# First loads on two queues, first unit's adapters inside the second unit, halves and last block reordered

## The chip, the cores and the metric

The kernel runs on one core of one Trainium2 chip. The metric is the device time of one execution in microseconds (us), from the first instruction to the last with what lies around them; lower is better. The engines are called here as in the profile: PE (TensorE, matmuls), DVE (VectorE), ACT (ScalarE), POOL (GpSimd) and SP (SyncE, which only begins transfers). ACT's queue can begin transfers too.

## The reference

```python
# x: (8, 256, 1024) float32; adapters chosen per sequence by itok_B_2_6 and itok_B_1_7
def lora_add(base, inp, A, B):                     # rank 16
    t = einsum('bri,bni->bnr', A[0][lora_indices], inp)
    return base + einsum('bor,bnr->bno', B[0][lora_indices], t) * 0.5
gate = lora_add(einsum('bnh,fh->bnf', x, W_gate), x, A_gate, B_gate)   # F = 2752
up   = lora_add(einsum('bnh,fh->bnf', x, W_up),   x, A_up,   B_up)
act  = silu(gate) * up
x = x + lora_add(einsum('bnf,hf->bnh', act, W_down), act, A_down, B_down)
x = x + einsum('bsi,oi->bso', x, weight) + bias + scale * lora(x)      # 1024 x 1024
```

## The kernel before

All products are float32 made of pairs: each operand is split into a high part (ACT writes it, rounded to the matmul's type) and a low part (DVE or POOL subtract the high part from the source), and PE multiplies high*high, high*low and low*high. So before a product can start, its weights (`W`) and its tokens (`X_B`, `X_T`) must have been loaded, turned by a DVE transpose, copied by ACT and subtracted by DVE or POOL.

The first phase makes `act`. The 2048 tokens go in two halves of 1024; each half runs over 22 units of 128 features (the last has 64). Twenty of the units of a half save products by sums and differences of quarter blocks (stages P1 to P7), for which DVE makes sums of tokens (`T1` to `T4`, `x_sum`) and of weights. The first two units of a half are multiplied plainly, since these sums aren't there yet: `first_unit` (banks a, b, c, d for gate and up, and both chunks of 512 tokens, with the tokens in two parts kq = 0 and 1 as they arrive) and `second_unit`. The first unit also multiplies the adapters' A matrices (`AG`) with the tokens. From that come the small matrices `Tm_g` and `Tm_u`: ACT copies one part (`t_copy`), DVE adds the other and masks (`t_sum`), ACT makes high parts (`t_high`), DVE low parts (`t_low`). The adapter stages E11, E21, E12 and E22 multiply them with `Bf` and close the banks. In the first unit these four stages come right behind its last product.

The tiles are loaded by SP into three rotating buffers `raw` in one written order (`raw_order`). A load waits until the item three places earlier has been turned, and takes 4 to 16 transfers: 4 for an x tile (`("x", half, n)`) or a gate or up tile (`("G", U)`, `("U", U)`), 16 for one pair of adapters A (`("Ag", half, p)`), 8 for B (`("b", half, n)`). SP also reads the adapters' indices from memory one by one (`batch_indices`); the eight indices and eight scale factors of the last layer are read behind `("b", 0, 0)`.

The second phase multiplies `act` with `W_down` in 11 blocks; in each block every pair of banks is added by DVE to `acc` (`add_down`). Before a pair can be multiplied again, its add must be done: (k, pr) is feature tile k for half pr, `t` the down adapters' A product. In the last block the adapters B (`Bd`, four of them; the last two serve the second half) and `Td` close each pair. The third phase multiplies with `weight` and stores; the last result's second chunk is stored by SP in 4 transfers.

PE, DVE, ACT and POOL each run their own instructions in the order in which the functions below issue them, and wait for each other by semaphores; nothing is reordered by a scheduler. In the rows L1843 is the matmul helper, L475 turns a weight tile, L536 an x tile, L581 a pair of A adapters, L592 a B tile, L567 is `x_sum`, L571 and L1729 are the low parts of tokens, L1725 the low part of weights, L613 and L616 `t_sum`, L1403 `t_high`, L622 `t_low`, L604 `b_low`, L821 and L832 turn and split `Bd`, L886 is the add of a bank pair, L904 `td_low`.

## Time and profile before

| | |
|---|---|
| median of 3 runs | 1707.95 us (1706.78 to 1709.65) |
| the profiled execution's own time | 1708.54 us |
| its span, first to last instruction | 1706.7 us |
| PE busy | 1631.3 us, 96% of the span |
| DVE busy | 1126.1 us, 66% |
| POOL busy | 668.2 us, 39% |
| ACT busy | 501.5 us, 29% |
| mean granted clock of PE | 0.985 of full speed |

The span is that of the profiled execution; 1.8 us of its time lie around it. Busy shares are means over the whole span. The page also cuts the span into 40 slices: PE is 90% busy or more in 35 of them, and below that in the first two, at the change of halves, near the last block and in the last one.

### The profile page before, as it was taken

The page shows a single profiled execution, that of the slowest core. Times are in us where ns is not written, and L with a number is a line of the kernel's source. Part 1 is how long each engine was busy: PE and PEld are TensorE (multiplying, and loading weights), DVE is VectorE, ACT ScalarE, POOL GpSimd, SP SyncE. Part 2 cuts the span into 40 slices and gives each one's busy share as a digit, 9 for nine tenths or more (in the row PEclk, how much of TensorE's full clock was granted, in tenths as well). Part 3 has the DMA queues.
Part 4 walks back from the last instruction along what each step waited for, and adds up shares of the span by engine and source line. Part 5 has one row for each costly group of instructions (what it writes and reads, how often), then busy time and mean ns, then how long its engine had stood idle before and what let it go on. Part 6 is the DMA issues. An engine that isn't in the chain of part 4 may idle for free.

```text
span 1706.7 us, 20952 instructions
## 1 busy us (share of the span) xinstructions
PE 1631.3 (96%) x7060; PEld 1320.1 (77%) x7060; DVE 1126.1 (66%) x1294; ACT 501.5 (29%) x833; POOL 668.2 (39%) x449
## 2 busy tenths in 40 slices
PE   4499999999997999999999999999999999899998
PEld 3378788888876788888888788888888887678886
DVE  3767777777768677777777565665555577765343
ACT  2343333333334433333433311111111122331100
POOL 3254444444444544444444533333233331541110
PEclk9799999999998999999999999999999999999999
DMA  6224344533442234335332662222222130103322
GB/s 132 60 78 102 103 126 113 149 88 92 113 111 67 77 103 125 116 102 163 91 90 89 177 221 78 77 78 60 68 76 78 58 69 25 25 21 78 74 46 59
DMA packets 218318, 156.13 MB, mean 91 GB/s; under 512 B 110884, under 2 KB 200356, under 8 KB 215460
## 3 DMA queue, kind: packets, MB, share of 16 engines
q1 hardware_dynamic: 171872, 115.97, 26.7%
q10 hardware_dynamic: 46212, 38.81, 7.1%
q8 instruction: 58, 0.95, 0.2%
q14 instruction: 48, 0.39, 0.1%
q0 software_dynamic: 128, 0.00, 0.0%
HBM read 115.38 MB, written 39.32 MB: 91 GB/s over the span
## 4 chain that ended last, share of the span: by engine, by line
PE 61%; DVE 2%; issue 1%; POOL 1%; ACT 0%; DMA 0%; SPq 0%; ACTq 0%; DVEq 0%
PE ps L1843 61%; POOL act L1768 0%; DVE acc L886 0%; POOL Wd L1776 0%; DMA raw<-in_x_dram 0%; POOL W L1725 0%; DVE tw_down L860 0%; DVE turned L821 0%; DVE tw_down L869 0%; DVE act_last L892 0%; DVE tw_down L899 0%; ACT W L1300 0%; DVE s L508 0%; DVE tw_down L866 0%; DVE tw_down L863 0%
## 5 line engine op out<-in xcount | busy, mean ns | idle before, releaser
L1843 PE MATMUL ps<-act,Wd 128*128 128x512 f32 x2016 | 463.3, 390 | 2.3 <-DVE acc L886 1.2
L1843 PE MATMUL ps<-X_T,W 128*128 128x512 f32 x1944 | 460.1, 392 | 5.6 <-DVE X_T L571 3.8
L1843 PE MATMUL ps<-X_B,W 128*128 128x512 f32 x1728 | 424.8, 395 | 22.2 <-POOL W L1725 15.3
L1843 PEld LDWEIGHTS ps<-act,Wd 128*128 128x128 f32 x2016 | 379.1, 188 | 83.0 <-DVE acc L886 1.6
L1843 PEld LDWEIGHTS ps<-X_T,W 128*128 128x128 f32 x1944 | 364.2, 188 | 89.1 <-DVE vbuf L636 8.2
L1843 PEld LDWEIGHTS ps<-X_B,W 128*128 128x128 f32 x1728 | 329.5, 191 | 96.2 <-POOL W L1725 14.2
L886 DVE TENSOR_TENSOR acc<-acc,ps 128x1024 f32<-128x1024 f32 x176 | 214.3, 1220 | 186.8 <-PE ps L1843 186.3
L1725 POOL TENSOR_TENSOR W<-s,W 128x512 fp32r<-128x512 f32 x156 | 208.8, 1339 | 237.9 <-ACT W L1300 237.9
L1725 POOL TENSOR_TENSOR W<-TG,W 128x512 fp32r<-128x512 f32 x88 | 131.8, 1499 | 205.8 <-ACT W L1300 205.8
L1300 ACT ACTIVATE W<-s 128x512 fp32r<-128x512 f32 x156 | 98.7, 632 | 281.0 <-PE ps L1843 275.3
L1768 POOL TENSOR_TENSOR act<-stage,act 128x1024 fp32r<-128x1024 f32 x42 | 100.6, 2415 | 175.2 <-ACT act L1518 175.2
L1843 PE MATMUL ps<-X1hi,Wo 128*128 128x512 f32 x512 | 141.4, 390 | 0.0
L1843 PEld LDWEIGHTS ps<-X1hi,Wo 128*128 128x128 f32 x512 | 96.1, 188 | 20.6
L1518 ACT ACTIVATE act<-stage 128x1024 fp32r<-128x1024 f32 x42 | 42.4, 1049 | 186.1 <-PE ps L1843 165.3
L630 DVE TENSOR_TENSOR qbuf<-p1buf,ps 128x512 f32<-128x512 f32 x38 | 26.1, 688 | 106.1 <-PE ps L1843 105.9
L1776 POOL TENSOR_TENSOR Wd<-turned,Wd 128x512 fp32r<-128x512 f32 x44 | 55.8, 1292 | 73.9 <-ACT Wd L1552 73.9
L1300 ACT ACTIVATE W<-TG 128x512 fp32r<-128x512 f32 x88 | 55.0, 628 | 88.1 <-PE ps L1843 78.4
L1843 PE MATMUL ps<-X1lo,Wo 128*128 128x512 f32 x256 | 80.3, 390 | 0.0
L604 DVE TENSOR_TENSOR Bf<-ts,Bf 32x256 fp32r<-32x256 f32 (+1 forms) x88 | 62.4, 709 | 26.3 <-ACT Bf L1384 24.4
L1725 POOL TENSOR_TENSOR W<-TU,W 128x512 fp32r<-128x512 f32 x46 | 60.5, 1318 | 38.6 <-ACT W L1300 38.6
L1384 ACT ACTIVATE Bf<-ts 32x256 fp32r<-32x256 f32 (+1 forms) x176 | 71.8, 408 | 1.5
L1776 POOL TENSOR_TENSOR Wo<-turned,Wo 128x512 fp32r<-128x512 f32 x16 | 21.8, 1380 | 120.8 <-ACT Wo L1552 120.8
(131 smaller groups left out, 1541.7 us busy)
## 6 DMA issues: line engine op xcount, KB each, us to landing
raw<-in_L_cond_W_gate_dram SPq DMA_DIRECT2D x168, 128.0 KB, 3.2
raw<-in_L_cond_W_up_dram SPq DMA_DIRECT2D x168, 128.0 KB, 3.2
stage<-act_scratch SPq DMA_DIRECT2D x21, 1024.0 KB, 5.1
raw<-in_x_dram SPq DMA_DIRECT2D x128, 128.0 KB, 3.2
raw<-in_L_cond_W_down_dram SPq DMA_DIRECT2D x88, 128.0 KB, 3.3
act_scratch<-c21buf ACTq DMA_DIRECT2D x42, 256.0 KB, 2.4
act_scratch<-vbuf ACTq DMA_DIRECT2D x42, 256.0 KB, 2.8
xt_scratch<-xt ACTq DMA_DIRECT2D x4, 2048.0 KB, 7.1
```

What stands on the lines that cost most here:

```text
L604: last = V.tensor_tensor(dst, src, hi.bitcast(F32), ALU.subtract)
L630: V.tensor_tensor(qbuf[:, :], p1buf[:, :], bank(U % 2, "b"), ALU.add).then_inc(q_done, 1)
L886: V.tensor_tensor(acc[pr][:, k, :], acc[pr][:, k, :], src[:, :], ALU.add).then_inc(b_added.up(s), 1)
L1300: A.activation(hi, src, ACT.Copy).then_inc(w_hi, 1)
L1384: last = A.activation(home, src, ACT.Copy)
L1518: A.activation(acts[t % 3][:, 0, cols], stage[t % 2][:, cols], ACT.Copy).then_inc(act_hi.up((t, pr)), 1)
L1725: G.tensor_tensor(low, src, hi.bitcast(F32), ALU.subtract).then_inc(w_lo, 1)
L1768: G.tensor_tensor(acts[t % 3][:, 1, cols], stage[t % 2][:, cols], acts[t % 3][:, 0, cols].bitcast(F32), ALU.subtract).then_inc(act_lo.up(( ...
L1776: last = G.tensor_tensor(low, src, hi.bitcast(F32), ALU.subtract)
L1843: return nc.tensor.matmul(dst, stationary, moving, start=start, stop=stop, skip_group_check=True)
```

## The change

The diff does the following.

- First loads: tiles G and U of unit 0 get buffers of their own (`raw_first`, where `Tm` lies later) and are begun by ACT's queue, while SP begins x tiles 0 to 3; the pair `("Ag", 0, 0)` comes behind them. For half 0 an A pair is loaded by 4 transfers of whole rows (4 KB a row) in place of 16 (1 KB a row), and DVE turns it by 8 transposes of 32 partitions in place of one of 128. SP reads only the two indices that it needs next, and the reads and loads for the last layer's factors move from behind `("b", 0, 0)` to behind `("b", 0, 3)`.
- First unit: its stages E11, E21, E12 and E22 are issued within the second unit, behind that unit's stage I11. `tw` holds both chunks, so that ACT copies both at once. DVE does all `t_sum` and then all `t_low`, and the first unit's silu and product with up (`plain_acts`) come in the second unit, on ACT behind the T4 tokens.
- Change of halves: x tiles 6 and 7 of half 1 are loaded and turned behind the half tile, in the first unit; x tiles 4 and 5 are turned behind `add_c12`; ACT does `copy_p1` ahead of `silu_second`.
- Last block: `Bd` 2 and 3 are turned and split within the last block rather than in and behind the block before it; `last_low(1)`, `td_first` and the turning of `Wo` and `Al` move as well.
- Last store: SP and ACT begin two of its four transfers each.

```diff
+        raw_first = {"G": at("raw_gate", 190464, [P, 1024]), "U": at("raw_up", 194560, [P, 1024])}
-        tw = at("tw", 180224, [Q, 2, TT])
+        tw = at("tw", 180224, [Q, 2, 2, TT])
...
-            order = [("x", 0, 0), ("x", 0, 1), ("G", 0), ("U", 0), ("Ag", 0, 0), ("x", 0, 2), ("x", 0, 3)]
+            order = [("x", 0, 0), ("x", 0, 1), ("x", 0, 2), ("x", 0, 3), ("Ag", 0, 0)]
...
+                    if h == 1:
+                        order += [("x", 1, 6), ("x", 1, 7)]
+                    order += [("Ag", h, 1)]
...
+                for w in range(2):
+                    for q in range(NQ):
+                        last = V.transpose(
+                            ts[q * Q:(q + 1) * Q, :].rearrange("p (k w i) -> p k w i", k=KT, w=2)[:, :, w, :],
+                            src[w * Q:(w + 1) * Q, q * HQ:(q + 1) * HQ].rearrange("p (k i) -> p k i", k=KT))
...
             def first_unit(U):
...
                 turn_tile(("U", U + 1))
+                b_low(U)
                 x_low(h, "T1", 0)
                 x_sum(h, "T1", 1)
+                for p in range(2):
+                    for w in range(2):
+                        t_sum(h, p, w)
+                for p in range(2):
+                    for w in range(2):
+                        t_low(h, p, w)
...
                 b_low(U + 1)
-                plain_acts(U)

             def second_unit(U):
                 h = U // UNITS
+                plain_acts(U - 1)
...
             def down_block(bb):
...
-                    elif bb == BLOCKS - 2 and n == 12:
+                    elif bb == BLOCKS - 2 and n == 11:
                         last_low(0)
-                        turn_item(("Bd", 2))
-                        bd_low(2)
-                    elif bb == BLOCKS - 2 and n == 14:
-                        turn_item(("Bd", 3))
-                    elif bb == BLOCKS - 2 and n in (15, 16):
-                        td_first(n - 15)
+                    elif bb == BLOCKS - 2 and n in (14, 15):
+                        td_first(n - 14)
 
             def last_block():
-                last_low(1)
-                bd_low(3)
                 for s in B_CLOSE[-18:]:
                     _, k, pr = s
                     add_down(s)
                     if (k, pr) == ("t", 0):
                         td_low(0, 0)
                         td_low(0, 1)
+                    elif (k, pr) == (0, 0):
+                        last_low(1)
+                    elif (k, pr) in ((1, 0), (3, 0)):
+                        turn_item(("Bd", 2 + k // 2))
+                    elif (k, pr) in ((2, 0), (4, 0)):
+                        bd_low(1 + k // 2)
...
         @block.scalar
         def _(eng):
             A = nc.scalar
...
+            for kind, w in (("G", w_gate), ("U", w_up)):
+                rows = w.rearrange("(g i) m -> i g m", i=Q)
+                for c in range(NQ):
+                    eng.dma_start(raw_first[kind][c * Q:(c + 1) * Q, :].rearrange("i (q m) -> i q m", q=NQ),
+                                  rows[:, 0:2 * NQ:2, c * HQ:(c + 1) * HQ]).then_inc(first_full[kind], 16)
...
                 x_high(h, "T2", 0)
+                b_high(U)
                 x_high(h, "T1", 1)
                 t_copy(h, 0)
-                b_high(U)
+                t_copy(h, 1)
                 t_high(h, 0)
-                x_high(h, "T2", 1)
-                t_copy(h, 1)
-                t_high(h, 1)
                 w_high(U + 1, "A11")
                 w_high(U + 1, "A12")
+                t_high(h, 1)
+                w_high(U + 1, "A21")
+                w_high(U + 1, "A22")
+                b_high(U + 1)
+                x_high(h, "T2", 1)
...
         @block.tensor
...
+            def first_adapters(U):
+                a, b, c, d = (bank(U % 2, n) for n in "abcd")
                 up(U, "E11", adapter(U, 0, 0, a))
                 up(U, "E21", adapter(U, 1, 0, b))
                 up(U, "E12", adapter(U, 0, 1, c))
...
                 both_chunks(U, 1, 1, (a, c))
+                first_adapters(U - 1)
                 both_chunks(U, 1, 2, (a, c))
```

How the order of instructions moves is seen on PE at the end of the first unit. `X_B` and `X_T` are tokens, `W_58` to `W_61` the four weight buffers, `Bf_82`/`Bf_84` and `Bf_83`/`Bf_85` the B adapters of the even and the odd units (numbered 82, 83 before and 84, 85 now). Before:

```order
L1843 MATMUL ps<-X_T_54,W_60 128x512 x6
L1843 MATMUL ps<-X_B_52,W_61 128x512 x6
L1843 MATMUL ps<-Tm_g,Bf_82 128x512
L1843 MATMUL ps<-Tm_u,Bf_82 128x512
L1843 MATMUL ps<-Tm_g,Bf_82 128x512
L1843 MATMUL ps<-Tm_u,Bf_82 128x512
L1843 MATMUL ps<-X_B_49,W_58 128x512 x12
L1843 MATMUL ps<-X_T_54,W_58 128x512 x12
L1843 MATMUL ps<-X_B_50,W_59 128x512 x12
L1843 MATMUL ps<-X_B_52,W_59 128x512 x12
```

And now:

```order
L1884 MATMUL ps<-X_T_54,W_60 128x512 x6
L1884 MATMUL ps<-X_B_52,W_61 128x512 x6
L1884 MATMUL ps<-X_B_49,W_58 128x512 x12
L1884 MATMUL ps<-X_T_54,W_58 128x512 x12
L1884 MATMUL ps<-Tm_g,Bf_84 128x512
L1884 MATMUL ps<-Tm_u,Bf_84 128x512
L1884 MATMUL ps<-Tm_g,Bf_84 128x512
L1884 MATMUL ps<-Tm_u,Bf_84 128x512
L1884 MATMUL ps<-X_B_50,W_59 128x512 x12
L1884 MATMUL ps<-X_B_52,W_59 128x512 x12
```

The four adapter products with `Tm` stood between the first unit's last product and the second unit's first; now 24 matmuls of the second unit's first weight tile (`W_58`) stand ahead of them.

On DVE the work around the start of the last block, before (`tw_down` with `ps` is the add of the first half's adapter product, `acc_87` is written by the last adds of the block ahead of it):

```order
L821 STREAM_TRANSPOSE turned_97<-raw_67 32x32x32
L886 TENSOR_TENSOR acc_87<-acc_87,ps 128x1024
L899 TENSOR_TENSOR tw_down<-tw_down,tacc 32x1024
L886 TENSOR_TENSOR acc_87<-acc_87,ps 128x1024
L899 TENSOR_TENSOR tw_down<-tw_down,tacc 32x1024
L886 TENSOR_TENSOR acc_87<-acc_87,ps 128x1024
L892 TENSOR_TENSOR act_last<-stage_89,act_last 64x1024
L832 TENSOR_TENSOR Bd_108<-turned_97,Bd_108 32x4x8x32
L860 TENSOR_TENSOR tw_down<-tw_down,ps 32x512
L863 TENSOR_TENSOR tw_down<-tw_down,ps 32x512
L869 TENSOR_TENSOR tw_down<-tw_down,pick_half 32x512
L860 TENSOR_TENSOR tw_down<-tw_down,ps 32x512
```

And now, from the add of (0, 0) to the second half's adapter product (`acc_88` is written by the first half's adds):

```order
L909 TENSOR_TENSOR acc_88<-acc_88,ps 128x1024
L915 TENSOR_TENSOR act_last<-stage_91,act_last 64x1024
L909 TENSOR_TENSOR acc_88<-acc_88,ps 128x1024
L844 STREAM_TRANSPOSE turned_98<-raw_67 32x32x32
L909 TENSOR_TENSOR acc_88<-acc_88,ps 128x1024
L855 TENSOR_TENSOR Bd_109<-turned_98,Bd_109 32x4x8x32
L909 TENSOR_TENSOR acc_88<-acc_88,ps 128x1024
L844 STREAM_TRANSPOSE turned_99<-raw_68 32x32x32
L909 TENSOR_TENSOR acc_88<-acc_88,ps 128x1024
L855 TENSOR_TENSOR Bd_110<-turned_99,Bd_110 32x4x8x32
L883 TENSOR_TENSOR tw_down<-tw_down,ps 32x512
L886 TENSOR_TENSOR tw_down<-tw_down,ps 32x512
```

The second low part of `act_last` and the transposes and low parts of the last two `Bd` stood ahead of the first half's adapter product; now they stand between the adds of the last block, ahead of the second half's adapter product.

## Rows read from the trace of the kernel before

**Rows 1.** Waits of the matmul engine over the span: us in total, times, longest:

```profile
PE ps L1843 <- DVE Tm_g L622: 26.2, 3, 11.9
PE ps L1843 <- POOL W L1725: 15.3, 3, 14.2
```

**Rows 2.** Timeline of PE, 0 to 125: start us, us busy, instructions, [idle before <-releaser]:

```profile
14.23 7.98 PE L1843 MATMUL ps<-X_B,W 128*128 128x512 f32 x24 [14.23 <-POOL W L1725]
...
58.88 1.52 PE L1843 MATMUL ps<-X_B,W 128*128 128x512 f32 x6
...
83.76 4.61 PE L1843 MATMUL ps<-X_B,W 128*128 128x512 f32 x12 [0.52 <-POOL W L1725]
...
98.36 0.73 PE L1843 MATMUL ps<-Tm_g,Bf 96*128 96x512 f32 x2 [1.83 <-DVE Bf L604]
...
110.33 2.93 PE L1843 MATMUL ps<-X_B,W 128*128 128x512 f32 x12
```

**Rows 3.** Timeline of the SP queue, 0 to 60:

```profile
13.45 3.85 SPq L1140 DMA_DIRECT2D raw<-in_L_cond_A_gate_dram  x8
...
53.02 5.13 SPq L1241 DMA_DIRECT2D scale_row<-ond_scaling_factors_dram  x8
```

**Rows 4.** Page, DMA issues: count, KB each, median us from issue to landing:

```profile
raw<-in_x_dram SPq DMA_DIRECT2D x128, 128.0 KB, 3.2
```

**Rows 5.** Busy time by window, DMA share in the last place but one:

```profile
4.00:12.00 8.00, 0.00 (x0) 0.00 (x0) 3.79 (x4) 2.02 (x3) 0.77 (x5) 1.00 1.11 212
```

**Rows 6.** Timeline of DVE, 0 to 70:

```profile
8.41 1.25 DVE L536 STREAM_TRANSPOSE xt<-raw 128x1024 f32<-128x1024 f32 x1 [1.56 <-DMA raw<-in_x_dram]
...
46.81 1.25 DVE L475 STREAM_TRANSPOSE TG<-raw 128x1024 f32<-128x1024 f32 x1 [0.99 <-DMA raw<-in_L_cond_W_gate_dram]
...
53.73 1.21 DVE L592 STREAM_TRANSPOSE ts<-raw 64x256 f32<-64x256 f32 x2
62.45 1.25 DVE L475 STREAM_TRANSPOSE TU<-raw 128x1024 f32<-128x1024 f32 x1 [7.51 <-DMA raw<-in_L_cond_W_up_dram]
...
67.71 0.68 DVE L613 TENSOR_TENSOR tw<-tw,ps 32x512 f32<-32x512 f32 x1 [0.47 <-ACT tw L1394]
```

**Rows 7.** Timeline of ACT, 50 to 75:

```profile
69.91 0.63 ACT L1403 ACTIVATE Tm_g<-tw 32x512 fp32r<-32x512 f32 x1
```

**Rows 8.** Timeline of POOL, 30 to 85:

```profile
32.30 2.46 POOL L1729 TENSOR_TENSOR X_B<-xt,X_B 128x1024 fp32r<-128x1024 f32 x1 [6.94 <-ACT X_B L1329]
...
82.35 3.49 POOL L1725 TENSOR_TENSOR W<-TG,W 128x512 fp32r<-128x512 f32 x2 [29.63 <-ACT W L1300]
```

**Rows 9.** Timeline of PE at the change of halves:

```profile
499.46 4.61 PE L1843 MATMUL ps<-X_B,W 128*128 128x512 f32 x12 [2.05 <-ACT p1buf L1337]
...
551.93 4.37 PE L1843 MATMUL ps<-X_B,W 128*128 128x512 f32 x12 [0.52 <-POOL W L1725]
...
577.42 2.93 PE L1843 MATMUL ps<-X_B,W 128*128 128x512 f32 x12
```

**Rows 10.** Timeline of DVE at the change of halves:

```profile
522.81 1.25 DVE L475 STREAM_TRANSPOSE TG<-raw 128x1024 f32<-128x1024 f32 x1 [0.16 <-DMA raw<-in_L_cond_W_gate_dram]
```

**Rows 11.** Timeline of PE in the last block:

```profile
1459.07 0.47 PE L1843 MATMUL ps<-Td,Bd 96*128 96x512 f32 x1 [3.70 <-DVE Td L904]
...
1460.87 2.76 PE L1843 MATMUL ps<-act,Wd 128*128 128x512 f32 x6
...
1480.42 1.64 PE L1843 MATMUL ps<-act,Wd 128*128 128x512 f32 x6 [1.21 <-DVE acc L886]
```

**Rows 12.** Timeline of DVE before and in the last block:

```profile
1420.18 3.98 DVE L845 STREAM_TRANSPOSE Ad_turned<-Ad_raw 32x64 f32<-32x64 f32 x16
...
1436.13 2.08 DVE L821 STREAM_TRANSPOSE turned<-raw 32x1024 f32<-32x1024 f32 x1
...
1461.11 1.22 DVE L886 TENSOR_TENSOR acc<-acc,ps 128x1024 f32<-128x1024 f32 x1 [0.89 <-PE ps L1843]
```

**Rows 13.** Timeline of the SP queue, last stores:

```profile
1702.32 1.99 SPq L439 DMA_DIRECT2D out_dram<-ct  x4
```

More of the change, by code:

```diff
@@ L210, in last_stage @@
         def last_stage(U):
-            return (U, stages_of(U % UNITS)[-1])
-        STAGES = [(U, s) for U in range(ALL) for s in stages_of(U % UNITS)]
+            return (U, "E22" if plain(U) else stages_of(U % UNITS)[-1])
+        STAGES = []
+        for U in range(ALL):
+            for s in stages_of(U % UNITS):
+                STAGES += [(U - 1, e) for e in ("E11", "E21", "E12", "E22")] if s == "first" else [(U, s)]
         pe_a = Order("pe_a", STAGES)
@@ L257, in raw_order @@
                 if h == 0 and u == FULL - 1:
-                    order += [("G", U + 2)] + [("x", 1, n) for n in range(4, 8)]
+                    order += [("G", U + 2), ("x", 1, 4), ("x", 1, 5)]
                 if h == 0 and u == FULL:
@@ L279, in dmas @@
                 return 8
-            if item[0] in ("Ag", "Al"):
-                return 16 if item[0] == "Ag" else 32
+            if item[0] == "Al":
+                return 32
+            if item[0] == "Ag" and item[1] == 1:
+                return 16
             return 8 if item[0] == "G" and half_tile(item[1]) else 4
@@ L430, in b_places, with store_out @@
             return src, homes[0], homes[1]
-        def store_out(eng, m, c):
+        def store_out(eng, m, c, qs=range(NQ)):
             k, pr = divmod(m, 2)
             eng.wait_ge(out_turned, (k // 2 * 2 + pr) * 2 + c + 1)
-            for q in range(NQ):
+            for q in qs:
                 col = q * HQ + (k - 1) * Q
@@ L460, in turn_tile @@
                 kind, U = item
-                src = take(item)
+                if U == 0:
+                    eng.wait_ge(first_full[kind], NQ * 16)
+                    src = raw_first[kind]
+                else:
+                    src = take(item)
                 if kind == "G":
@@ L1086, in _, with batch_indices @@
         def _(sp):
-            def batch_indices(table, rows):
-                return [sp.value_load(indices[:, table * NB + b:table * NB + b + 1], min_val=0, max_val=rows - 1)
-                        for b in range(NB)]
+            l0, l1 = {}, {}
+            def batch_indices(table, batches):
+                found, rows = ((l0, a_gate.shape[1]), (l1, a_out.shape[0]))[table]
+                for b in batches:
+                    found[b] = sp.value_load(indices[:, table * NB + b:table * NB + b + 1], min_val=0,
+                                             max_val=rows - 1)
             def slot(item):
@@ L1138, in load_ag @@
                         rows = a_all[bass.ds(l0[h * 4 + 2 * p + b], 1), :, :].rearrange("o r m -> (o r) m")
+                        if h == 0:
+                            first = w * Q + b * R
+                            sp.dma_start(buf[first:first + R, :], rows).then_inc(filled, 16)
+                            continue
                         for q in range(NQ):
@@ L1232, in _ @@
                         sp.wait_ge(indices_loaded, 2 * 16)
-                        l0 = batch_indices(0, a_gate.shape[1])
+                    first = 4 * item[1] + 2 * item[2]
+                    batch_indices(0, range(first, first + 2))
                     load_ag(item)
@@ L1268, in _ @@
                     load_bo(item)
-            store_out(sp, 2 * KT - 1, 1)
+            store_out(sp, 2 * KT - 1, 1, range(0, 2))
             for c in range(2):
@@ L1388, in t_copy @@
                 wait_stage(eng, h * UNITS, f"A{p}")
-                if p == 1:
-                    eng.wait_ge(t_lo, 4 * h + 2)
-                elif h == 1:
-                    eng.wait_ge(act2_done, UNITS)
+                if h == 1:
+                    for c in range(2):
+                        eng.wait_ge(act_stored[c], 16 * UNITS)
                 for w in range(2):
-                    A.activation(tw[:, w, :], bank(1, "dc"[p])[(2 * w + 1) * Q:(2 * w + 2) * Q, :], ACT.Copy
+                    A.activation(tw[:, p, w, :], bank(1, "dc"[p])[(2 * w + 1) * Q:(2 * w + 2) * Q, :], ACT.Copy
                                  ).then_inc(t_copied, 1)
@@ L1691, in _ @@
                         store_out(eng, m, 1)
+                    else:
+                        store_out(eng, m, 1, range(2, NQ))
                 if pr == 1 and k + 2 < KT:
```

94 lines of the change are left out of this document (45 added, 49 removed).

## The prediction

> **What bounds the kernel now.** I read the waits of PE first, then PE's timeline where they fall, then the queue and the engine that PE waited for there. The matmuls keep PE busy for nearly the whole span; what can still be won is idle time and half-clock time, and it lies in four places. The longest waits are for `Tm_g`, 26.2 us in three waits, and for weights, 15.3 us in three [rows 1]. On the timeline: PE starts at 14.23; the last product of the first unit ends at 60.4 (58.88 + 1.52); the second unit starts only at 83.76, and the third at 110.33 [rows 2]. A unit there is 100 matmuls, some 23 us at full clock, since 12 in the third unit take 2.93 and the last overlaps the next (about 0.23 each). In the same place of the second half the second unit starts at 551.93 and the third at 577.42 [rows 9]. In the last block PE waits 3.70 for `Td`, then runs slowly (6 matmuls in 2.76 rather than 1.4), and waits once more at 1480.42, 1.21 for an add of DVE [rows 11]. Last come four stores begun one behind the other in 1.99 [rows 13].
>
> **The first loads.** SP and ACT would begin loads at once. The window from 4 to 12 has a DMA share of 1.11 and 212 GB/s [rows 5]: the sixteen DMA engines are full already. x tiles 0 and 1 and tiles G and U are 2 MB, 9.9 us at that rate, whichever queue begins them. So x tile 1, turned at 8.41 before [rows 6], now shares the engines with G and U and lands somewhere between there and 12; I take 11, because two queues with equal shares leave it until nearly the end of the 2 MB. The Trainium skill says the same (DMA: Bandwidth & Descriptors, "Issuing engines are not separate DMA queues"): transfers begun by several engines interleave on the same sixteen, and only issue time is saved. By that rule alone this edit gives nothing; by the row it costs 2 to 3 us at PE's start (14.23, now about 16.5), and gives it back only if what comes behind is earlier.
>
> What comes behind hangs on DVE. From 11 it does seven operations of 1.2 (1.25 for a tile [rows 6]): x1, G, a low part, U, a low part, x2, x3: 19.5. Then the A pair in 8 pieces. Sixteen pieces of 64 columns take 3.98, 0.25 each [rows 12]; two of 256 columns take 1.21, 0.6 each [rows 6]; one instruction for all can't be under half a tile's 1.25. That bounds the eight by 0.6 and 4.8; I take 3.3, between the two piece rows: 22.8. ACT's three copies (0.63 for 512 columns [rows 7], so an estimated 1.1 for 1024) bring 25.6; POOL now does a token low part first, 2.46 [rows 8], then AG's 1.3: 29.3. The second pair waits for that, since both use `ts`: 32.6. Now SP loads x6, x7 and G of unit 1: 12 transfers at 0.48 (8 in 3.85 [rows 3]) and 3.2 to land [rows 4] make 41.5. Before, DVE turned that G at 46.81 [rows 6]. This step is 5.3 us earlier.
>
> **From G of unit 1 to its first product.** DVE turns G, makes two token sums and turns B: 46.81 to 54.94, 8.1 us [rows 6]. I keep that: 49.6. Before, DVE then sat 7.51 until U landed at 62.45, behind the eight scale factors, 5.13 of SP's queue [rows 3, 6], and their index reads. Those are now behind `b` 3, and U (begun by about 45) is there. From U to the first product was 21.3 us (62.45 to 83.76), because `tw` held one chunk: the second chunk's copy, sum, mask, high and low parts came behind the first's, and W's high part behind them all on ACT. Now: U 1.2, `b_low` with its wait 1.3, two token operations 2.4, ACT's high part and first copy 1.7, four small DVE operations at 0.7 [rows 6] 2.8, the last two high parts 1.3 and W's 0.6 [rows 7], W's low part 1.7 (3.49 for two [rows 8]): 13.0. The second unit starts at 62.6 rather than 83.76, 21.2 earlier. PE's first unit ends before that: x7 is turned at about 41, two low parts of POOL (2.5 or more each) last to 47, and 32 matmuls behind them, 7.4, end at about 55. So it still idles 7 us and starts at half clock, as the 4.61 for 12 matmuls shows for now too [rows 2].
>
> **The rest of the second unit.** Before, it took 26.6 (83.76 to 110.33). The four adapters lie in it now (0.9), and PE then waits for `b_low` of unit 1, as it did for 1.83 at 98.36 [rows 2]: DVE has the same sums and one or two low parts more ahead of it, so some 15 us from the unit's start where it was 14.6. From there to the third unit are 12.0 (98.36 to 110.33). That gives 26.9; the third unit starts at 89.5, 20.8 earlier. The silu and product of unit 0 have moved into this unit, ahead of the next unit's weight sums, and `b_high` now ends about 3 us later against the third unit. By my count the add that its stage P7 needs is 2.1 late. 18.7 are left.
>
> **The change of halves.** x tiles 6 and 7 no longer stand ahead of `second_act`, and `p1buf` is copied first: PE's 2.05 wait and the half clock behind it (4.61 for 12 rather than 2.93) go [rows 9]. But the path that decides is DVE's again: G of the second unit is turned at 522.81 [rows 10]; it can be perhaps 1 earlier, since SP's order of loads up to it is the same. From there 8.1 and 13.0, as above, give 542.9 rather than 551.93, then 26.9: 569.8 against 577.42 [rows 9], 7.6 earlier. P7 loses 0.7: 6.9.
>
> **The last block.** The 3.70, the half clock and some waits go, since DVE has only the adapter product's six operations ahead of `Td`. PE arrives at (0, 1) at about 1472.5. That product needs the add of (5, 0), and DVE now does in between, from 1455.9: six adds of 1.22, `last_low` 1.2, two `Bd` transposes of 2.08 [rows 12], their low parts 2.4, two waits of 1.1 for ACT's part, and six small operations 4.3: 21.6. So PE waits until 1477.5 where it went on at 1480.42 [rows 11], and after 5 us of idleness it again runs at half clock; the present stretch lost 1.4 on 6 matmuls [rows 11], so some 2.4 altogether. Gain 0.6. The stall moves.
>
> The Trainium skill's clock rule (TensorE: Matmul & The Clock Gate, "Part 1: The HAM clock gate") puts PE at 1.2 GHz after idling and back at 2.4 GHz when busy. It would leave this gain at 0.6; without it the gain would be 3.0.
>
> **The last store.** Two transfers on SP rather than four: 1.0 [rows 13].
>
> **The sum.** 18.7 + 6.9 + 0.6 + 1.0 = 27.2. The profiled execution took 1708.5, 0.6 over the median of the three runs, so 1681.3.
>
> **Rivals.**
> 1. More is won. For: x1 lands at 9, the A pair turns in 2 rather than 3.3 (twice), P7 doesn't wait (2.8) and the last block loses no clock (2.4). 2 + 2.6 + 2.8 + 2.4 = 9.8 gives 1671.5. Against: each is a wait that I could derive from rows. 0.2.
> 2. The Vector path is longer. x1 at 12, eight pieces at 0.6 (3 us for both pairs), token sums slowed by POOL's low parts by 2 at each half, and the waits at P7 longer than 2 so that they too end in half clock (1.7 each): 1 + 3 + 4 + 3.4 = 11.4 gives 1692.7. For it: from 46.81 to 54.94 lie three operations that elsewhere take 1.25 and the B pair's 1.21 [rows 6], 5.0 in all, and they took 8.1, so DVE is slowed beside others here. 0.2.
> 3. The loads give nothing and only the order does: the step of 5.3 is lost, 1686.6. This lies in the forecast's own range. The Trainium skill's sentence above points this way.
> 4. Slower than before: the 38 ordinary units get longer, because every later load lies in another of the three `raw` buffers and the factor loads (some 10 us of queue with their reads) now come in unit 5. It needs 0.7 us in each unit to eat 27; the factors alone could cost at most their own 10, once. Nothing in the rows sets one buffer apart, and the queue idles most of a unit. 0.03, and 0.02 for no change.
> The forecast, 1675 to 1689, has 0.55.
>
> **The range.** With rivals 1 and 2 to their middles, 1671 to 1694. Differences under 0.2% (3.4 us) of this kernel can't be told from none.
>
> **What the new profile would show.** PE's first matmul later than 14.23, by about 2; x1 turned at about 11; the second unit's first product at 60 to 66 and the third unit at 87 to 94; waits of PE for `Tm` near zero and a wait for W of some 7 in their place; a wait at the third unit's fourth stage; no wait for `Td`, but one of 4 to 6 for an add of DVE near 1450, and half clock behind it; the ordinary units as before. I am wrong if PE waits for A products beyond 30, if the second unit starts after 70, or if the last block's wait is gone.

## The result, and the profile after

The changed kernel took 1692.10 us (median of four runs, 1689.88 to 1692.88) against 1707.59 for the kernel before (four runs): ratio 0.9905, 95% interval 0.9888 to 0.9923. That is 15.5 us less where the sum gave 27.2. It is inside the range of 1671 to 1694, but 10.8 above the number and above the 1675 to 1689 to which the forecast had given 0.55. The profiled executions, on which the rest goes, stand at 1708.54 and 1689.88, their spans at 1706.7 and 1688.1: 18.6 less. The profiled one is the fastest of the four. In three of the runs below (`ag_four`, `one_queue`, `ends_back`), in which PE, DVE and ACT keep this stretch's order, PE waited 2.1 at P7 and went on at half clock, where this trace has 0.49 and full clock; whether the three slower executions of the changed kernel did the same is not shown, since they have no trace. "Half clock" is PE's granted clock of 1.2 GHz in place of 2.4: 12 matmuls take 2.9 us at full clock and up to 5.5 (at 529.81 below, granted clock 0.50) where the clock is half.

PE's waits in the changed kernel, by line and by what ended them (total, times, longest):

```profile
PE ps L1884 <- POOL W L1763: 30.0, 3, 16.7
PE ps L1884 <- POOL AG L1772: 7.1, 2, 5.9
PE ps L1884 <- DVE acc L909: 6.1, 2, 5.5
PE ps L1884 <- DVE Bf L627: 3.7, 2, 2.3
PE ps L1884 <- DVE X_B L585: 1.9, 1, 1.9
...
PE ps L1884 <- DVE qbuf L653: 1.4, 2, 0.9
PE ps L1884 <- DVE vbuf L659: 1.3, 2, 0.7
```

The 26.2 for `Tm` [rows 1] are gone and the waits for W are 30.0 rather than 15.3. There is a small wait for `qbuf`, the add that stage P7 needs, in each half; the forecast had charged it with 2.1 and 0.7. PE's timeline of the start:

```profile
64.20 4.58 PE L1884 MATMUL ps<-X_B,W 128*128 128x512 f32 x12 [8.23 <-POOL W L1763]
...
80.21 0.74 PE L1884 MATMUL ps<-Tm_g,Bf 96*128 96x512 f32 x2 [2.31 <-DVE Bf L627]
80.79 4.51 PE L1884 MATMUL ps<-X_B,W 128*128 128x512 f32 x12
...
93.78 2.93 PE L1884 MATMUL ps<-X_B,W 128*128 128x512 f32 x12
...
102.64 3.01 PE L1884 MATMUL ps<-X_T,W 128*128 128x512 f32 x12 [0.49 <-DVE qbuf L653]
...
109.49 3.06 PE L1884 MATMUL ps<-X_T,W 128*128 128x512 f32 x12 [0.66 <-DVE vbuf L659]
...
115.59 2.90 PE L1884 MATMUL ps<-X_B,W 128*128 128x512 f32 x12
```

Against [rows 2]: the second unit starts 19.56 earlier (64.20 for 83.76), the third 16.55 earlier (93.78 for 110.33), and the fourth, at 115.59, 15.1 earlier. So the second and the third unit each give some back. The change of halves and the last block, same columns, to be held against [rows 9, 11]:

```profile
481.66 3.01 PE L1884 MATMUL ps<-X_B,W 128*128 128x512 f32 x12 [0.69 <-ACT p1buf L1373]
...
494.35 4.34 PE L1884 MATMUL ps<-X_B,W 128*128 128x512 f32 x18 [1.86 <-DVE X_B L585]
...
507.12 0.70 PE L1884 MATMUL ps<-X_T,AG 128*128 128x512 f32 x2 [1.18 <-POOL AG L1772]
...
529.81 5.46 PE L1884 MATMUL ps<-X_B,W 128*128 128x512 f32 x12 [5.12 <-POOL W L1763]
...
545.79 0.74 PE L1884 MATMUL ps<-Tm_g,Bf 96*128 96x512 f32 x2 [1.36 <-DVE Bf L627]
...
557.74 2.93 PE L1884 MATMUL ps<-X_B,W 128*128 128x512 f32 x12
```

```profile
1453.87 0.63 PE L1884 MATMUL ps<-Td,Bd 96*128 96x512 f32 x2
1460.02 2.93 PE L1884 MATMUL ps<-act,Wd 128*128 128x512 f32 x6 [5.53 <-DVE acc L909]
```

The 2.05 is 0.69 and has no half clock behind it. There are waits at 494.35 and 507.12; in the place of the first the kernel before waited 1.75, the second was not there. The last block has no wait for `Td` any more and one of 5.53 instead.

Where the 18.6 come from is a subtraction of start times of the same instructions in the two traces:

```
                                       before   changed   earlier
fourth unit, P1                        130.73    115.59     15.14
22nd unit, P1                          494.51    478.07     16.44
second half, fourth unit, P1           597.84    580.00     17.84
last block, its first product         1447.03   1428.80     18.23
first product with Wo                 1503.19   1484.45     18.74
end of the span                       1706.7    1688.1      18.6
```

So the start gave 15.1, the ordinary units 1.7 (three waits of PE for `vbuf`, 0.80 and 0.53 in the first half and 0.34 in the second, fell away), the change of halves 1.4, the last block 0.5, and the last store nothing (0.1 the other way).

### The profile page after: what moved, and what is told of

It reads as the page before. It is cut to its first block, busy times and chain, and to the rows that moved or that the text cites. A ratio compares the mean times of both kernels' runs of the same rounds, so it can differ in the third digit from the quotient of the medians.

```text
span 1688.1 us, 20911 instructions
## 1 busy us (share of the span) xinstructions
PE 1626.5 (96%) x7060; PEld 1318.2 (78%) x7060; DVE 1135.1 (67%) x1308; ACT 500.6 (30%) x833; POOL 668.9 (40%) x449
## 4 chain that ended last, share of the span: by engine, by line
PE 63%; DVE 1%; POOL 1%; issue 1%; ACT 0%; ACTq 0%; DVEq 0%
PE ps L1884 63%; POOL act L1810 0%; POOL Wd L1818 0%; DVE turned L844 0%; DVE acc L909 0%; ACT Bd L1602 0%; POOL W L1763 0%; DVE tw_down L892 0%; DVE tw_down L883 0%; ACT W L1336 0%; DVE TU L489 0%; DVE ct L1025 0%; DVE turned L839 0%; DVE s L515 0%; DVE c21buf L672 0%
## 5 line engine op out<-in xcount | busy, mean ns | idle before, releaser
L653 DVE TENSOR_TENSOR qbuf<-p1buf,ps 128x512 f32<-128x512 f32 x38 | 26.1, 687 | 106.1 <-PE ps L1884 106.0
```

Of the source, the lines that this page charges most:

```text
L653: V.tensor_tensor(qbuf[:, :], p1buf[:, :], bank(U % 2, "b"), ALU.add).then_inc(q_done, 1)
```

## Experiments

There are two theories of the two starts. One, formed on the traces: between the second unit's tile G and the third unit's stage P7 there is a chain on DVE, with work of ACT in it, that ends in the add L653, and this chain, not PE's first product of the second unit, sets the time at both starts. Small operations of DVE are slow while POOL works, which makes the chain longer. Its rival: the first product sets it, the forecast's view, and the rest of the second unit only has single waits that can be taken away one by one. The expectations of the first four runs below were written from the rival's view; from `q_ahead_b_early` on they state the chain. Each "measured" is the median of four runs (five for the last kernel), and its ratio is against the kernel before, run beside it; rows come from one profiled run each. By the forecast's own measure differences under 3.4 us can't be told from none.

**The adapters back ahead of the second unit.** (All else as changed.)

```
-  return ["A0", "A1", "c", "d"]                     # u == 0
+  return ["A0", "A1", "c", "d", "E11", "E21", "E12", "E22"]
-  return ["I11", "first", "I12", ...]
+  return ["I11", "I12", ...]
```

> The changed kernel with one part undone: PE does the four adapter products of the first unit ahead of the second unit's first product again; all else is as changed. Theory: the first product must then wait for DVE's last t_low, which ended at 69.7 and 535.3 in the changed kernel, so it starts at about 70.6 and 536.2 rather than 64.20 and 529.81. The wait for Bf (2.31 and 1.36) and the half clock behind the first of them go, since that low part is done when PE comes. The third unit starts 3 later in the first half and 4 in the second: 1699 us, 1697 to 1701. Rival: the third unit is set by ACT's and DVE's weight sums and not by PE's order, so that PE only waits in another place: 1692 to 1693.

Measured 1691.78 us, ratio 0.9908 [0.9891, 0.9924]: no difference to the changed kernel. The first product did start late, at 71.88 rather than 64.20, and P7 had no wait at all. The add for P7 came at 103.36, 1.5 later than in the changed kernel, and 1.2 of that was there already at tile G. So 7.7 us of PE's start were worth nothing: the first half of my expectation held and its price fell; the rival named there was right, that PE only waits in another place.

**The scale factors back in front.** `if item == ("b", 0, 3)` is `("b", 0, 0)` again.

> The changed kernel with one part undone: the index reads and eight loads of the scale factors stand behind the first half's first B tile in SP's queue again, ahead of U of the second unit. Theory: with the reads they take some 7 to 10 us of the queue, U of the second unit is turned at 57 to 60 rather than 50.32, and as DVE's token sums, the copies and W's high part all stand behind it, the second unit starts 7 to 9 later. One half only: 1700 us, 1698 to 1702. Rival: the two waits that this path ends in (8.23 for W) are ended by other work, and U has slack: below 1694.

Measured 1697.39 us, ratio 0.9939 [0.9923, 0.9956]: 5.3 slower than the changed kernel. Tile U was turned at 57.66 rather than 50.32, the first product came at 70.88, 6.7 later, and the add for P7 as much. The wait for U is on the chain, and this is the one edit of the start whose worth is shown by itself. I had put it at 7 to 9.

**Weights' high parts behind.** ACT's order in the first unit.

```
   w_high(U + 1, "A11")
-  w_high(U + 1, "A12")
   t_high(h, 1)
-  w_high(U + 1, "A21")
-  w_high(U + 1, "A22")
   b_high(U + 1)
+  w_high(U + 1, "A12") ... "A21" ... "A22"
```

> The changed kernel with ACT's order in the first unit altered: the high parts of the second unit's A12, A21 and A22 stand behind both t_high and behind b_high of the second unit, so that POOL makes their low parts after DVE's four t_low and not beside them. Theory (DVE's small operations are slowed by POOL's beside them): t_low take 0.7 each, apart from the first, rather than 1.64 to 1.78; everything behind them on DVE is 3 earlier, b_low of the second unit among it, so that PE's wait of 2.31 for Bf, the half clock behind it (1.7) and the wait of 1.36 in the second half go: 1687 us, 1685.5 to 1689. Rival (they are slowed by ACT, which writes the same tiles, or by their own form): t_low stay at 1.7 and the time at 1691 to 1693, or above if A12 now comes late.

Measured 1691.48 us, ratio 0.9903 [0.9887, 0.9920]: the same. DVE's timeline of that run, and POOL's beside it:

```profile
63.87 1.64 DVE L645 TENSOR_TENSOR Tm_g<-tw,Tm_g 32x512 fp32r<-32x512 f32 x1
65.44 0.67 DVE L645 TENSOR_TENSOR Tm_u<-tw,Tm_u 32x512 fp32r<-32x512 f32 x1
...
66.65 0.67 DVE L645 TENSOR_TENSOR Tm_u<-tw,Tm_u 32x512 fp32r<-32x512 f32 x1
67.35 3.45 DVE L585 TENSOR_TENSOR X_T<-xs,X_T 128x1024 fp32r<-128x1024 f32 x2
70.90 2.13 DVE L581 TENSOR_TENSOR xs<-xt,xs 128x1024 f32<-128x1024 f32 x1
72.95 3.65 DVE L581 TENSOR_TENSOR xt<-xt 128x1024 f32<-128x1024 f32 x2
```

```profile
63.17 1.80 POOL L1763 TENSOR_TENSOR W<-TG,W 128x512 fp32r<-128x512 f32 x1 [13.97 <-ACT W L1336]
68.00 1.72 POOL L1763 TENSOR_TENSOR W<-TG,W 128x512 fp32r<-128x512 f32 x1 [3.02 <-ACT W L1336]
69.68 4.51 POOL L1763 TENSOR_TENSOR W<-TU,W 128x512 fp32r<-128x512 f32 x2
```

In the changed kernel the same stretch of DVE reads:

```profile
67.91 1.78 DVE L645 TENSOR_TENSOR Tm_u<-tw,Tm_u 32x512 fp32r<-32x512 f32 x1
69.72 2.36 DVE L585 TENSOR_TENSOR X_T<-xs,X_T 128x1024 fp32r<-128x1024 f32 x2
72.18 1.23 DVE L581 TENSOR_TENSOR xs<-xt,xs 128x1024 f32<-128x1024 f32 x1
73.33 2.55 DVE L581 TENSOR_TENSOR xt<-xt 128x1024 f32<-128x1024 f32 x2
```

Three `t_low` fell from 1.76 to 0.67 (POOL was idle from 64.97 to 68.00), as the theory said: it is POOL's low parts beside them that slow them. But POOL's work only moved behind them, and there the pair of token low parts took 3.45 rather than 2.36, the sum 2.13 rather than 1.23, the pair of sums 3.65 rather than 2.55: 3.1 of the 3.3 won are back. The Trainium skill (SBUF — State Buffer, "SBUF: two separate sides") says that DVE operations with two SBUF inputs and POOL's that read SBUF hold one pair of ports by turns, the other fully blocked. The trace agrees that the two slow each other: what one order saved the other paid, and a `b_low` took 3.81 in the changed kernel beside POOL's low parts (at 96.68) and 0.85 at 79.31, with POOL idle.

**`b_low` of the second unit early**: right behind the four `t_low`.

> The changed kernel with b_low of the second unit right behind the four t_low on DVE, ahead of the token sums and low parts that stood before it. Theory (the wait for Bf and its half clock are what the late b_low costs): it ends at 71 rather than 80.2, the waits of 2.31 and 1.36 and the 1.7 of half clock go, t_low stay at 1.7: 1687 us, 1685.5 to 1689. Rival: the token sums behind it are now 0.9 later, and PE waits for them or for the weight sums of the third unit instead: 1690 to 1693.

Measured 1694.95 us, ratio 0.9921 [0.9904, 0.9937]: 2.9 more than the changed kernel, too little to call it slower, but not the 5 less of the expectation. The wait for `Bf` did go, and this took its place:

```profile
104.72 4.62 PE L1884 MATMUL ps<-X_T,W 128*128 128x512 f32 x12 [4.00 <-DVE qbuf L653]
```

4.00 in P7, then half clock. One operation more ahead of the token sums made the chain 1.1 longer (0.8 in the second half); the wait that it removed lay beside the chain. This speaks against the view of single waits: one was taken away, and nothing was won.

**The same, with `b_low` of the third unit behind the add.** DVE: `sums`, `plain_acts(U)`, then `add_q(U + 1)`, `b_low(U + 1)`.

> The run b_low_early with one thing more: b_low of the third unit, which took 3.8 there rather than 0.85 beside POOL's token low parts and stood ahead of the add that PE's stage P7 waits for, now stands behind that add. Theory (in both halves a chain on DVE, from G of the second unit to that add, sets the time; waits taken from PE ahead of it only come back as a wait in P7): the add is 3.8 earlier, at 99 rather than 102.6 in the first half, the waits of 4.0 and 4.0 in P7 go, and with the wait for Bf gone too the third unit's P7 starts at 100 to 101: 1687 us, 1685 to 1689. Rival: the next thing on the chain takes its place (adapters of the third unit, the v add): 1691 to 1695.

Measured 1690.30 us, ratio 0.9892 [0.9875, 0.9908]. Against the run before it 4.7 are won: the add started at 99.31 rather than 103.97. The time is 3.3 above the expectation, since PE now waits 1.68 for a low part of W at P7 and 1.54 for the v add. Against the changed kernel the 1.8 less can't be told from none.

**Tokens ahead.** ACT and DVE in the first unit.

```
   b_high(U)                          # ACT
-  x_high(h, "T1", 1)
   t_copy(h, 0); t_copy(h, 1)
+  w_high(U + 1, "A11")
   t_high(h, 0)
-  w_high(U + 1, "A11") ...
   ...
-  x_low T1 0; x_sum T1 1             # DVE, ahead of the eight t_sum
   t_sum x4; t_low x4
+  b_low(U + 1); x_low T1 0; x_sum T1 1
```

> The changed kernel with ACT's and DVE's order in the first unit altered: ACT copies both chunks and makes the high part of the second unit's A11 as soon as PE lets it, ahead of a token high part and of t_high; DVE does the eight t_sum and four t_low and b_low of the second unit ahead of the token sums. PE's first product of the second unit then starts at about 58.5 rather than 64.20. Theory (DVE's chain to the add of the third unit decides, and this change takes no work from it, only 1 to 2 of its idle time): PE waits in P7 instead, for 6 or more, and the time is 1691 to 1695. Rival (the first product decides, as the prediction had it): each half gains what the first product gains, 5 and more, and 1680 to 1684 comes out.

Measured 1690.04 us, ratio 0.9891 [0.9875, 0.9908].

```profile
59.26 4.61 PE L1884 MATMUL ps<-X_B,W 128*128 128x512 f32 x12 [2.36 <-DVE tw L636]
...
88.94 5.34 PE L1884 MATMUL ps<-X_B,W 128*128 128x512 f32 x12 [4.08 <-issue]
...
102.22 3.04 PE L1884 MATMUL ps<-X_T,W 128*128 128x512 f32 x12 [2.48 <-DVE qbuf L653]
```

PE's first product is 4.9 earlier than in the changed kernel and P7 0.4. The time is 1 us under the theory's 1691 to 1695 and far from the rival's 1680 to 1684. PE idles 4.08 and 2.48 instead. For the 4.08 the profile names nothing; POOL's low part of the third unit's first weights ended at 88.70, 0.2 ahead, and is the likely one. What I call the chain can be read off all runs as one number, from G of the second unit on DVE (its start) to the add L653 (its start); the last six rows are of kernels described further down:

```
                     first half          second half
kernel before        46.81 -> 116.88 70.07   522.81 -> 583.98 61.17
changed              42.72 -> 101.89 59.17   507.98 -> 566.29 58.31
adapters_first       43.92 -> 103.36 59.44   509.49 -> 567.77 58.28
weights_behind       43.55 -> 102.63 59.08   509.55 -> 567.68 58.13
tokens_ahead         43.40 -> 101.48 58.08   507.16 -> 565.98 58.82
b_low_early          43.65 -> 103.97 60.32   510.73 -> 569.86 59.13
factors_early        43.13 -> 108.56 65.43   515.10 -> 573.37 58.27
q_ahead_b_early      43.59 ->  99.31 55.72   508.49 -> 563.07 54.58
ag_four              42.84 -> 102.30 59.46   505.85 -> 564.13 58.28
one_queue            41.79 -> 101.29 59.50   507.84 -> 566.20 58.36
ends_back            43.63 -> 103.04 59.41   509.65 -> 567.95 58.30
no_chain_fix         43.24 -> 102.01 58.77   504.67 -> 563.45 58.78
all_four             43.54 ->  97.53 53.99   506.55 -> 559.93 53.38
gap_fill             43.53 ->  97.63 54.10   503.12 -> 556.67 53.55
```

In eight of these kernels it is 58.1 to 59.5 in both halves, though PE's first product moves by up to 12.6 us. It is longer where U comes late (`factors_early`, first half) or where an operation is put ahead of the token sums (`b_low_early`), and shorter where the slowed `b_low` of the third unit is taken from ahead of the add. In `all_four` and `gap_fill` the add itself waits 4.45 and 4.63 for PE, so there PE's own work ends the stretch.

The chain is not DVE's work alone. In the changed kernel DVE stands still for over 3 us twice in it:

```profile
81.39 1.28 ACT L1379 ACT_TABLE_LOAD   x1
...
83.37 0.69 DVE L698 TENSOR_TENSOR c21buf<-s1buf,ps 128x512 f32<-128x512 f32 x1 [3.21 <-issue]
...
96.68 3.81 DVE L627 TENSOR_TENSOR Bf<-ts,Bf 32x256 fp32r<-32x256 f32 x2 [5.04 <-ACT Bf L1420]
...
101.89 0.69 DVE L653 TENSOR_TENSOR qbuf<-p1buf,ps 128x512 f32<-128x512 f32 x1
```

In the first gap ACT makes the high parts of T4, loads a table and does unit 0's silu; in the second it works up to `b_high` of the third unit. This fits `b_low_early`: `b_low` of the second unit cost nothing behind the token sums, where it fell into time in which DVE had to wait for ACT anyway, and lengthened the chain when it stood ahead of them (the gap is 4.09 there). Taking ACT's part out was not tried.

**A pairs of the second half in 4 transfers** (the branches on `h == 1` for the 16 transfers and the one transpose taken out).

> The changed kernel with the A pairs of the second half loaded like those of the first: 4 transfers rather than 16, and turned in 8 pieces rather than one. Theory (at the change of halves the loads on SP's queue decide): the queue spends 1.7 rather than 7.8 on each pair, so the first pair is turned some 4 earlier than 491.25, PE's waits of 1.86 for X_B and 1.18 for AG go, and G of the second unit, turned at 507.98, is some 8 earlier, less twice 2.8 more on DVE for the pieces: the second unit's first product comes 4 to 6 earlier than 529.81 and the stage P7 of the third unit as much: 1687 us, 1685 to 1689. Rival: DVE is what is short there, the pieces cost it 5.6, and G comes no earlier: 1692 to 1696.

Measured 1687.83 us, ratio 0.9875 [0.9858, 0.9891]: 4.3 less than the changed kernel by the medians, 2.0 by the two profiled runs, and the two intervals still touch. The queue spends 1.78 on a pair, the wait for AG is gone, that for `X_B` is 0.90, and G is turned at 505.85; since this run came to the change of halves 0.9 later, that is 3.0 earlier, and P7 is 3.0 earlier too. It is not the 8 less 5.6 of the expectation: the second pair's load now starts only at 492.42, when DVE has turned what lay in its buffer, and G's at 498.23 for the same reason. Both theories had a part of it, and the gain itself rests on the trace: 3.0 at G and the same 3.0 at P7.

**One queue.** G and U of the first unit begun by SP behind x tiles 0 and 1.

> The changed kernel with one part undone: the first G and U tiles, still in their own buffers, are begun by SP behind x tiles 0 and 1, as before, and not by ACT at once. Theory (the sixteen DMA engines carry what is asked for, and beginning loads by two queues only shares them differently): x tile 1 is turned at 8.4 to 9 rather than 11.5 to 12.3, but G and U come 4 later on SP's queue and push x tiles 2 and 3 and the first A pair back by their 4 of issue; the first pair's AG, on which PE waits until 29.8, is 3 to 4 later, and so is G of the second unit: 1695 us, 1693 to 1697. Rival (issue is hidden, as when the loads give nothing): 1691 to 1693, with PE's first matmul 2 earlier.

Measured 1690.71 us, ratio 0.9901 [0.9884, 0.9917]: not slower than the changed kernel. x tile 1 was turned at 8.44, PE started at 14.40 rather than 16.69, and G of the second unit came at 41.79, not later but 0.9 earlier. My expectation of 4 later fell: the queue got to the first A pair at 14.02 rather than 12.90, and DVE turned it at 19.12 rather than 19.93, because DVE had been let go sooner. Beginning the loads by two queues is worth nothing here. The Trainium skill (DMA: Bandwidth & Descriptors, "Issuing engines are not separate DMA queues") says that transfers begun by several engines share the same sixteen DMA engines and that only issue time is saved; this run agrees.

**The two ends back**: the last block's order, and all four last stores by SP.

> The changed kernel with two parts undone, in places that do not touch: the last block's order on DVE, ACT and POOL as before, and the last chunk's four stores all begun by SP. Theory (the stall only moved, and the last transfers are bound by what they move, not by their issue): the waits of 3.7 for Td and 1.2 for the add come back, the wait of 5.5 goes, and the first Wo product comes 0.5 later against the last block's start; from the last transpose to the end stays at 4.4 to 4.6: 1692.5 us, 1691.5 to 1694. Rival (the stores were worth the 1.0 forecast, or the block more): 1694 to 1696.

Measured 1691.87 us, ratio 0.9897 [0.9880, 0.9913].

```profile
1430.59 0.63 PE L1884 MATMUL ps<-act,Ad 128*64 128x512 f32 x2
...
1442.63 0.47 PE L1884 MATMUL ps<-Td,Bd 96*128 96x512 f32 x1 [3.70 <-DVE Td L927]
...
1444.44 2.76 PE L1884 MATMUL ps<-act,Wd 128*128 128x512 f32 x6
...
1464.01 1.67 PE L1884 MATMUL ps<-act,Wd 128*128 128x512 f32 x6 [1.12 <-DVE acc L909]
...
1486.80 0.63 PE L1884 MATMUL ps<-X1hi,Wo 128*128 128x512 f32 x2
```

From the block's start (1430.59) to the first `Wo` product 56.21, where the changed kernel has 55.65 (1428.80 to 1484.45): the order is worth 0.56. From the end of the last transpose to the end of the span 4.4, where the changed kernel has 4.55: the stores are worth nothing, although SP's issue is 1.98 here and 0.87 there. The two together are 0.2 by the medians, which is none.

**Four things together.** `ag_four`, `tokens_ahead`, in the last block `Bd` 3 turned behind the add of (5, 0), and `b_high`, `b_low` of the third unit behind the copy and the add for P7.

> Four things together: the second half's A pairs in 4 transfers (ag_four); tokens and weights ahead in the first unit (tokens_ahead); b_high and b_low of the third unit behind the copy of P1 and the add that its stage P7 needs; and in the last block the turn and low part of the fourth Bd tile behind the add that frees the pair for (0, 1), so that PE's wait of 5.5 there and the half clock behind it go. Theory (the chain on DVE and ACT to the third unit's add decides, 3.8 of it the slowed b_low): P7 is reached at 99.5 to 100.5 rather than 102.64 in the first half, and 2.5 earlier in the second, on top of what ag_four gave; in the last block (0, 1) starts 4 earlier and then waits for the Bd tile, so that 1.5 to 3 are gained there: 1681 us, 1678 to 1684. Rival: POOL's low part of S3, behind the two token low parts, ends the chain anyway, and the last block's adapter waits the rest: 1685 to 1688.

**The same without the last of these.**

> The run all_four without its third part: b_high and b_low of the third unit stand ahead of that add again. Theory: PE waits 2.5 for it in P7 of the third unit in each half, so this takes 4 to 6 more than all_four. Rival (POOL ends the chain): the same as all_four to 1.5.

Measured 1686.44 us, ratio 0.9876 [0.9859, 0.9892], for `all_four`, and 1683.39, ratio 0.9856 [0.9840, 0.9873], for `no_chain_fix`. Both expectations fell: the first came out in its rival's range, and the second is 3.0 less where 4 to 6 more were expected. P7 has no wait in the first half and 1.10 in the second, as forecast, but then comes

```profile
102.69 2.89 PE L1877 MATMUL ps<-X_B,W 128*128 128x512 f32 x12
...
109.42 5.49 PE L1877 MATMUL ps<-X_T,W 128*128 128x512 f32 x12 [3.38 <-DVE vbuf L652]
```

where `no_chain_fix` waits 3.01 in P7 and nothing for the v add. DVE's row shows why: after the add the turn of G waited 2.82 for POOL, and `b_low`, 2.86 long beside POOL, stood behind it.

```profile
97.53 0.69 DVE L646 TENSOR_TENSOR qbuf<-p1buf,ps 128x512 f32<-128x512 f32 x1 [4.45 <-PE ps L1877]
101.04 1.25 DVE L487 STREAM_TRANSPOSE TG<-raw 128x1024 f32<-128x1024 f32 x1 [2.82 <-POOL W L1756]
102.32 2.86 DVE L620 TENSOR_TENSOR Bf<-ts,Bf 32x256 fp32r<-32x256 f32 x2
...
108.69 0.68 DVE L652 TENSOR_TENSOR vbuf<-p1buf,ps 128x512 f32<-128x512 f32 x1
```

The last block: PE waits 2.33 rather than 5.53 ahead of (0, 1). Half clock still follows, a little later (the granted clock is 0.73 in `all_four` from 1458.65 to 1461.80), but from the block's start to the first `Wo` product it is 52.1 in both runs rather than 55.65: 3.6 won, more than the 1.5 to 3 expected.

**`b_low` into that gap.** One line of `all_four` moved: `b_low(U)` ahead of `turn_tile(("G", U + 1))`.

> The run all_four with b_low of the third unit one place earlier on DVE: between the add for P7 and the turn of the next G, where DVE sat idle 2.82 in all_four because that turn waits for a low part of POOL. Theory (all_four was slower because that b_low, 2.86 long there, and the idle time stood ahead of the v add, for which PE then waited 3.38 and 3.42 and ran 12 matmuls in 5.49): the v add ends at about 106.5 rather than 109.4, PE's wait ahead of P4 falls to 1 or less in each half with full clock behind it, and P7 keeps its place: some 5 less in each half than all_four, and less than no_chain_fix by 2 to 3 in each: 1678 us, 1675 to 1681. Rival (the turn of G waits for POOL, and POOL is slowed by the b_low beside it, so that the v add comes as late as before): 1683 to 1687.

Measured 1679.87 us (five runs, 1678.90 to 1680.14), ratio 0.9838 [0.9825, 0.9852].

```profile
59.19 3.01 PE L1877 MATMUL ps<-X_B,W 128*128 128x512 f32 x12 [2.42 <-DVE tw L629]
...
88.86 5.46 PE L1877 MATMUL ps<-X_B,W 128*128 128x512 f32 x12 [5.69 <-issue]
...
107.61 3.04 PE L1877 MATMUL ps<-X_T,W 128*128 128x512 f32 x12 [1.48 <-DVE vbuf L652]
```

The expectation, 1675 to 1681, held. The v add's wait is 1.48 at full clock, and 1.54 in the second half. That is 6.6 less than `all_four`, 12.2 less than the changed kernel, 27.4 less than the kernel before; the intervals of this ratio and of the changed kernel's do not meet.

## Why the prediction was right in sign and short by ten

**What became of the 27.2.** By the traces the start is short of the forecast by 3.6, the change of halves by 5.5, the last block by 0.1 and the end by 1.1; the ordinary units gave 1.7 that nobody had forecast. That is 8.6, and the profiled execution lies another 2.2 under the median: 10.8. So the time is inside the range only by the room that the second rival had made, and the 1.7 that nobody had forecast helped.

**Bound.** Idle and half-clock time in four places: right, and the gain came from them, 1.7 from ordinary units apart.

**First loads.** x1 turned at 11 (11.48), PE's start 16.5 (16.69), the eight pieces 3.3 (3.53 and 3.57), AG 29.3 (its wait ended at 29.80), G 41.5 (42.72): each row bears its step out, 1.2 late by G. (Three copies at 1.1 are 3.3, not the 2.8 that the forecast added; with them its 29.3 would have been the 29.8 measured.) G is 4.1 earlier rather than 5.3, and the stretch from G to the add 10.9 shorter (70.07 to 59.17); together they are the start's gain. `one_queue` shows that none of it is from the second queue. `factors_early` shows that U no longer behind the factors gives 6.3 of the 10.9 in the trace and 5.3 by the medians, the largest single part. The other 4.6 come from the new order, and which of its moves gives them was not separated; nor was the A pair in 4 transfers tested in the first half.

**From G to the first product.** 21.1 forecast, 21.48 measured, 21.83 in the second half: right.

**The rest of the second unit.** 26.9 forecast, 29.58 and 27.93 measured. This step failed in size, the first time by 1.0 because `b_low` ended 16.0 after the unit's start rather than 15 (four `t_low` at 1.76), and by 1.6 because the 2.31 of waiting was followed by half clock (12 matmuls in 4.51), which the forecast did not charge. The 2.1 put on P7, a count for which the forecast showed no rows, was 1.4: the third unit took 21.81 (93.78 to 115.59) where it took 20.40. Start: 1.2 + 0.4 + 2.7 - 0.7 = 3.6 of the 18.7 are missing, 15.1 are there.

**What was wrong in kind.** The sum added up PE's rows, first product, rest of the unit, wait at P7, as if the first decided. The experiments show that the last decides: `adapters_first` and `tokens_ahead` move the first product by +7.7 and -4.9 and the time by nothing that can be told. The forecast got near by luck in this: DVE's chain was earlier for the same reasons as the first product, the U tile and G, so that adding up the wrong path gave nearly the right number.

**The change of halves.** 6.9 forecast, 1.4 measured; here the prediction failed most. The step: "it can be perhaps 1 earlier, since SP's order of loads up to it is the same". It isn't: x tiles 6 and 7, which stood ahead of both A pairs, now stand between them. The first pair is begun 3.0 earlier against the second half's start, but G's load 1.9 later (503.02 for 517.57), and relative to that start G was turned 1.6 later (522.81 less the 16.4 that the kernel was ahead is 506.4; it was turned at 507.98), 2.6 off. Then 0.7 from G to the first product, 1.0 in the rest of the unit, 1.1 in P7 and P4: the 5.5 that are missing, but for rounding. The 2.05 with its half clock went as forecast; by the time that G was turned it was taken back. That the loads of the A pairs matter there `ag_four` shows: 3.0 back. The new place of x tiles 6 and 7 was not undone by itself.

**Last block.** 0.6 forecast, 0.51 and, by undoing it, 0.56 measured; the stall moved, 5.53 for the 5 forecast, half clock behind it, 2.93 for 6 matmuls.

**Last store.** 1.0 forecast, nothing measured, twice. The issue time did fall, from 1.98 to 0.87, but the end does not hang on it: from the last transpose to the end it is 4.4 to 4.55 either way. What lands last there stays open.

**Rivals.** The second, the longer Vector path, was nearest in number (1692.7) and in part in kind: contention is there, in `t_low` rather than in the token sums, and half clock too. The fourth did not come: ordinary units take what they took.

## To carry to other kernels

Find the last thing that a stretch waits for and walk back from that, not forward from the first idle time: here each wait that was taken away ahead of it came back as another. Measure the chain as one number over several variants; if it stays constant while PE's waits move about, it is probably the bound, and an edit that shortens it has to show it. Of a reordering on an engine that shares something with another, ask who pays at the new place, and use gaps where the engine waits anyway.

## What the hardware showed that was not expected

Four small DVE operations took 1.64 to 1.78 beside POOL's low parts and 0.67 without; moved off, the same 3 us appeared on other DVE operations. The wait of 1.86 at the second half's first unit is in nine runs the same to 0.02, yet PE ran the 18 matmuls behind it in 4.34 (changed kernel, `ends_back`, `tokens_ahead`, `one_queue`) and in 5.96 to 5.98 (`adapters_first`, `weights_behind`, `b_low_early`, `q_ahead_b_early`, `factors_early`): equal waits of some 2 us were followed by full clock (2.4 GHz), or by a stretch partly at half (1.2 GHz; a granted clock of 0.71 in `adapters_first` from 495.70 to 501.60). In the latter runs the wait for AG behind it was absent, so that the clock there cost little or nothing. Why one and not the other was not settled.
